# Row-wise stages of a decoder layer in 13 tiles of up to 126 rows instead of 16 tiles of 100

## The chip, the cores and the metric

The kernel runs on one core of one Trainium2 chip, as one program. The metric is device time in microseconds (us), lower is better. The engines are PE (TensorE, matrix products; PEld is its weight load), DVE (VectorE), ACT (ScalarE), POOL (GpSimd) and SP (SyncE, which here only issues DMAs). Each engine runs its own list of instructions in order and waits on semaphores.

## What is computed

One pre-norm decoder layer on 16 batches of 100 rows, width 512, in fp32:

```
x = x + self_attention(layernorm(x))        # 16 heads of 128, rotary, RMS-normed q and k, sink
x = x + cross_attention(layernorm(x), ctx)  # 16 heads of 32, keys and values from ctx
x = x + moe(layernorm(x))                   # RMS norm, router, 4 of 32 experts, plus a shared expert
```

The causal mask leaves only the first 100 of the 361 context rows in use. Attention works within a batch; layer norms, projections, the router and the shared expert work on each row by itself.

## The kernel before, in words

The program has four parts. **Joining**: two weight matrices of the output projection are multiplied into one per head (`join`), in 16 pieces. **Steps**: a software pipeline of 16 steps, one per batch (`step(b)` on every engine; steps 2 to 14 are a hardware loop in `pipeline`). **Behind the steps**: the leftovers of the pipeline, woven by hand into the shared expert. **Experts**: the 32 routed experts, two blocks of 128 gathered rows each, whose results are added into the output rows by indirect DMAs.

In step b the engines do the self-attention of batch b (stage A), the input norm, queries and keys of batch b+1 (stage Q), the cross attention of batch b-1 (stage X) and the norm, router and rank of batch b-2 (stage C). The order within a step is written out by hand for each engine. On PE it is: transposes of keys and queries (L532, L543), scores (L549, L552), `cross_queries` (transposed h2, context keys and values, the query product L453), `ln1_columns`, `cross_products`, `compress`, `queries` (L425, which waits until the cross scores have been copied out, `sx`), transposed probabilities and their product with the values (L584, L589), `normed_columns`, the output projection `project` (48 products of 512 columns, L382 to L384), with `router`, `cross_transposed` (L493, waits for `px_norm`), `cross_values` (L504) put between its last heads, `ranks`, and `cross_out` (L520), which waits for the copied columns `oxT`. Then the next step's first transpose waits for the scaled keys (`k_scaled`).

Most products with fp32 precision are made as three products of "high" and "low" halves (`split_product`). The high half is a copy by ACT, the low half a subtraction by DVE; both must be there before PE can start. Behind the steps the shared expert's weights ("sg", "su", "sd") and the normed rows in columns ("h0" to "h3", four groups of 400 rows) are split in this way (`split_high`, `split_low`); the first inner product of the shared expert waits for sg and h0, and its second half for su. Inner product n of 16 (`shared_inner`: PE makes gate and up products, ACT the SiLU, DVE the product, ACT the high and DVE the low half) feeds `shared_outer(g)`, 12 products of 512 columns for each tile of rows; DVE adds the kept base row (`shared_rows`) into one of two tiles `ytile`, and POOL stores it.

On DVE the parts that matter are the four scaled copies of the scores, max, shift, sum and norm of the softmax (L1272 to L1300), `cross_shifted` and `cross_normed` (L1189 to L1200), `rotate` (L1151 to L1158), `norms` (L1163, whose power of -0.5 POOL computes at L1483), `routed` (L1205 to L1229), the addition of the projected row (L1320) with its statistics, `scale_keys` (L1168) and `ranked` (L1234 to L1245). All 1600 rows stay in on-chip memory as `resid`, 16 tiles of 100 rows. POOL issues four indirect DMAs for each tile (`listed`), which write row numbers into the expert lists.

## Time and profile before

| what | value |
|---|---|
| median of 3 runs | 1219.54 us (1204.15, 1219.54, 1219.91) |
| the profiled execution | 1210.05 us |
| its span, first to last instruction | 1208.3 us |
| mean granted clock of PE | 0.983 of full speed |
| PE busy | 1146.3 us, 95% |
| DVE busy | 811.5 us, 67% |
| ACT busy | 595.0 us, 49% |
| first step starts, last step ends | 68.5 us, 726.2 us |
| first product of the first `shared_outer` | 783.1 us |

Times in the trace are us from the start of the span. A busy share is an average over parts with different limits. A row of the timeline merges neighbouring instructions of one kind; the bracket at its end says how long the engine was idle before it and what ended that.

### The profile page before, as it was taken

To read this page: it belongs to the slowest core of one execution; us is meant where nothing else is said; L and a number is where in the kernel's file an instruction comes from. 1 tells how busy PE (TensorE), PEld (TensorE's weight loads), DVE (VectorE), ACT (ScalarE), POOL (GpSimd) and SP (SyncE) were. 2 spreads that over 40 slices of the span, in tenths; PEclk is the share of its full clock that TensorE was granted. 3 is DMA by queue.
4 is the path that set the end of the run, shared out by engine and by line. 5 is a ranking of instruction groups with operands and counts; after the bars stand their busy time and mean duration, and the time that the engine had idled before them with its cause. 6 is when DMAs were issued, how large, how long until landed. Compare 5 with 4: busy or idle time off the path is not lost. (4 is left out here: it accounts for less than half of the span.)

```text
span 1208.3 us, 21017 instructions
## 1 busy us (share of the span) xinstructions
PE 1146.3 (95%) x7761; PEld 905.7 (75%) x7762; DVE 811.5 (67%) x1392; ACT 595.0 (49%) x1404; POOL 359.2 (30%) x279
## 2 busy tenths in 40 slices
PE   6989999999999999999999989899799999999993
PEld 3457677767776777777677758788699999898992
DVE  1355798789778978887898868532356666666660
ACT  1334564456446544654554435311156666666661
POOL 0011112211221122112122202222226676667653
PEclk9999999999999999999999988999989999999997
DMA  8450000000000000000000005122669999999964
GB/s 276 141 178 11 1 10 9 16 14 9 9 16 14 9 9 14 9 9 16 14 9 9 17 24 191 44 88 67 229 195 266 261 263 265 263 257 240 268 103 53
DMA packets 62598, 117.59 MB, mean 97 GB/s; under 512 B 10932, under 2 KB 14564, under 8 KB 62388
## 3 DMA queue, kind: packets, MB, share of 16 engines
q1 hardware_dynamic: 44820, 82.46, 20.2%
q0 software_dynamic: 17728, 34.44, 14.5%
q8 instruction: 33, 0.54, 0.2%
q14 instruction: 17, 0.14, 0.0%
HBM read 93.55 MB, written 28.13 MB: 101 GB/s over the span
## 5 line engine op out<-in xcount | busy, mean ns | idle before, releaser
L1483 POOL TENSOR_TENSOR rall<-qkv_var,phalf 100x17 f32<-100x17 f32 x16 | 49.1, 3071 | 404.1 <-DVE qkv_var L1163 404.1
L1561 POOL DMA_INDIRECT out_rows<-work,idx x64 | 119.6, 1868 | 110.0 <-issue 55.0
L382 PE MATMUL QS<-xh,wh 128*128 128x256 f32 x512 | 148.6, 290 | 0.0
L383 PE MATMUL QS<-xl,wh 128*128 128x256 f32 x512 | 146.0, 285 | 0.0
L384 PE MATMUL QS<-xh,wl 128*128 128x256 f32 x512 | 145.8, 285 | 0.0
L382 PE MATMUL W<-wch,oth 128*100 128x512 f32 x256 | 105.1, 410 | 0.0
L383 PE MATMUL W<-wcl,oth 128*100 128x512 f32 x256 | 100.6, 393 | 0.0
L384 PE MATMUL W<-wch,otl 128*100 128x512 f32 x256 | 100.4, 392 | 0.0
L382 PEld LDWEIGHTS QS<-xh,wh 128*128 128x128 f32 x512 | 99.4, 194 | 1.2
L383 PEld LDWEIGHTS QS<-xl,wh 128*128 128x128 f32 x512 | 99.4, 194 | 1.2
L384 PEld LDWEIGHTS QS<-xh,wl 128*128 128x128 f32 x512 | 99.2, 194 | 0.0
L1431 DVE TENSOR_TENSOR wl<-raw,wh 128x2048 fp32r<-128x2048 f32 (+1 forms) x48 | 84.5, 1761 | 12.1 <-ACT wh L799 10.9
L1483 POOL TENSOR_TENSOR rstd<-var,phalf 100x1 f32<-100x1 f32 (+1 forms) x48 | 30.2, 630 | 178.7 <-DVE var L1124 121.4
L1452 DVE TENSOR_TENSOR work<-work,QS 128x256 f32<-128x256 f32 x64 | 26.7, 417 | 72.5 <-ACT work L1063 54.5
L799 ACT ACTIVATE work<-W 128x400 f32<-128x400 f32 (+1 forms) x132 | 55.8, 508 | 31.8 <-PE W L584 31.7
L799 ACT ACTIVATE wh<-raw 128x2048 fp32r<-128x2048 f32 (+1 forms) x48 | 70.7, 1472 | 0.0
L453 PEld LDWEIGHTS W<-h2T,w_x 128*128 128x128 f32 x512 | 59.6, 192 | 8.1 <-ACT h2T L799 5.0
L1043 ACT ACTIVATE work<-W,wcol 128x512 f32<-128x512 f32 x64 | 40.5, 686 | 45.0 <-PE W L384 45.0
L1513 POOL DMA_INDIRECT expert_lists<-tok,slot x56 | 57.1, 1020 | 16.3 <-issue 16.3
L453 PE MATMUL W<-h2T,w_x 128*128 128x100 f32 x512 | 59.4, 274 | 0.0
L520 PE MATMUL W<-w_x,oxT 128*100 128x512 f32 x128 | 58.4, 599 | 0.0
L799 ACT ACTIVATE work<-QS 100x400 f32<-100x400 f32 (+1 forms) x76 | 41.7, 616 | 33.7 <-DVE work L1155 23.3
(223 smaller groups left out, 2880.9 us busy)
## 6 DMA issues: line engine op xcount, KB each, us to landing
raw<-in_w SPq DMA_DIRECT2D x24, 1024.0 KB
raw<-in_w SPq DMA_DIRECT2D x24, 512.0 KB
work<-in_w SPq DMA_DIRECT2D x8, 1024.0 KB
work<-in_w SPq DMA_DIRECT2D x8, 512.0 KB
hx_rows<-h3x SPq DMA_DIRECT2D x16, 212.5 KB
h_columns<-h3s SPq DMA_DIRECT2D x16, 200.0 KB, 1.9
h3T<-h_columns SPq DMA_DIRECT2D x4, 800.0 KB, 15.5
out_rows<-ytiles POOLq DMA_DIRECT2D x16, 200.0 KB, 2.5
```

Of the source, the lines that this page charges most:

```text
L382: mm(dst, ah, bh, start=start, stop=False)
L383: mm(dst, ah, bl, start=False, stop=False)
L384: return mm(dst, al, bh, start=False, stop=stop)
L453: last = mm(wb[1][:, T * i:T * (i + 1)], w_q[:, 512 * k + P * i:512 * k + P * (i + 1)], h2T[:, T * k:T * (k + 1)], start=k == 0, stop=k == ...
L520: last = mm(wb[3][0:T, :], oxT[:, T * k:T * (k + 1)], w_out[:, 512 * k:512 * (k + 1)], start=k == 0, stop=k == KC - 1)
L799: return fn(dst, src, ACT.Copy)
L1043: last = fn(Y[e % 2][:, 512 * j:512 * (j + 1)], wb[j][:, :], ACT.Copy, scale=wcol[e % RING][:, j:j + 1])
L1431: tt(wl[e % 2][:, c], slots_w[e % RING][:, c], wh[e % 2][:, c].bitcast(fp32), ALU.subtract).then_inc(m.wl, 1)
L1452: tt(ea[:, 256 * v:256 * (v + 1)], et[:, 256 * v:256 * (v + 1)], QS[:, 1280 + 512 * v:1536 + 512 * v], ALU.mult).then_inc(m.act, 1)
L1483: return nc.gpsimd.tensor_tensor(out=dst, in0=src, in1=phalf[:, 0:src.shape[1]], op=ALU.pow)
L1513: nc.gpsimd.indirect_dma_start(table, on_rows(slot[:, k:k + 1]), tok[:, :], None)\
L1561: nc.gpsimd.indirect_dma_start(out, on_rows(idx[:, NE * j + e:NE * j + e + 1]), Y[e % 2][:, 512 * j:512 * (j + 1)], None, compute_op=ALU.a ...
```

## The change

Everything that works on each row by itself behind the self-attention now takes tiles that cross the borders of batches. Five batches make four tiles of 124, 126, 126 and 124 rows; fifteen batches make 12 tiles, and the sixteenth is a tile of 100 rows, 13 in all (`pieces`). A tile can only be made once all its batches are there, so `tile_at(b)` gives the tile that is finished by batch b, and none for b = 0, 5 and 10. In step b now:

- self-attention of batch b, as before; its output columns go into a buffer of two batches (`oth3`, `otl3`), and `project` runs for `tile_at(b)`;
- norm 2 and the query product for `tile_at(b - 1)`, whose result ACT copies out in the pieces that belong to each batch;
- cross attention of batch b-2 (`context`, `cross_products` and so on), and `cross_out` for `tile_at(b - 2)`;
- norm 3, router and ranks for `tile_at(b - 3)`.

The hardware loop is gone, all steps are written out. Instead of `resid` there is a ring of four tiles; SP loads x twice (by batch for norm 1, by tile for the sum), stores each base tile to memory and loads the first nine back behind the steps. Constants for rows 100 to 125 are filled with 23 small DMAs (`spread`), behind the others, and POOL waits for all of them before its first step. POOL now issues the list DMAs of a tile ahead of the power for the next tile's norm 3. The shared expert's four groups have 3, 3, 3 and 4 tiles (376, 374, 374 and 476 rows). Its intermediate tile is one buffer (`joint`), so SiLU n waits for low half n-1. Behind the steps two cross attentions, two `cross_out` and three routers are left, instead of one, one and two.

```diff
+TT = 126
+NT = 13
+def tiles_of(b):
+    if b < 0:
+        return 0
+    return NT if b >= NB - 1 else 4 * (b // 5) + b % 5
+def tile_at(b):
+    return tiles_of(b) - 1 if 0 <= b < NB and tiles_of(b) > tiles_of(b - 1) else None
...
@@ tensor, step @@
+                c = b - 2
+                queried, listed, done = tile_at(b - 1), tile_at(b - 3), tile_at(b)
...
-                    project(b, range(0, 12))
+                if done is not None:
+                    project(done, b, range(0, 12))
...
+                if c >= 0:
+                    pe.wait_ge(s.px_norm, c + 1)
...
+                    cross_transposed(qb)
...
+                if tile_at(c) is not None:
+                    pe.wait_ge(s.oT, 4 * b + 4)
+                    cross_out(tile_at(c), c)
...
@@ gpsimd @@
-            pool.wait_ge(s.pad_st, 48)
-            pipeline(pool, step)
+            pool.wait_ge(s.pad_st, 48 + 16 * SPREAD)
+            for b in range(NB):
+                step(b)
...
@@ scalar, behind the steps @@
+            cross_exp(NB - 1)
+            shared_inner(2)
+            shared_inner(3)
+            columns_out(NT - 2)
...
@@ vector, behind the steps @@
-            normed(NB - 2, NB)
+            cross_shifted(NB - 2)
+            normed(NT - 3, NT)
             split_low("sg")
             split_low("h0")
-            cross_shifted(NB)
+            cross_normed(NB - 2)
+            routed(NT - 3)
             split_low("su")
```

**Place 1: DVE, just behind the steps.** `w_sgl`, `w_sul` are low halves of shared weights, `h3l` those of a group of rows; `mxx` belongs to `cross_shifted`, `denx` and `rx` to `cross_normed`, `lgs` starts `routed`. Before:

```order
L1181 SCALAR_TENSOR_TENSOR h3x<-work,rstd_90,normw 100x512
L1183 SCALAR_TENSOR_TENSOR resid<-work,rstd_90,resid 100x512
L1356 TENSOR_TENSOR w_sgl<-w_sh,w_sgh 128x2048
L1356 TENSOR_TENSOR h3l<-h3T,h3h 128x1600
L1189 TENSOR_REDUCE mxx<-work 100x16
L1191 TENSOR_TENSOR work<-work,mxx 100x1600
L1356 TENSOR_TENSOR w_sul<-w_sh,w_suh 128x2048
L1196 TENSOR_REDUCE denx<-work 100x16
```

After:

```order
L1384 TENSOR_REDUCE mxx<-work 100x16
L1386 TENSOR_TENSOR work<-work,mxx 100x1600
L1369 TENSOR_SCALAR work<-ring,mv_82 126x512
L1376 SCALAR_TENSOR_TENSOR h3x<-work,rstd_88,normw 126x512
L1378 SCALAR_TENSOR_TENSOR ring<-work,rstd_88,ring 126x512
L1567 TENSOR_TENSOR w_sgl<-w_sh,w_sgh 128x2048
L1567 TENSOR_TENSOR h3l<-h3T,h3h 128x1504
L1391 TENSOR_REDUCE denx<-work 100x16
L1393 RECIPROCAL rx<-denx 100x16
L1395 TENSOR_TENSOR work<-work,rx 100x1600
L1402 COPY lgs<-W 126x32
```

`cross_shifted` now stands ahead of norm 3 and of the first two splits, and `cross_normed` and the whole of `routed` (11 instructions from L1402 on) stand between the split of h0 and that of su.

**Place 2: DVE, around the first output rows of the shared expert.** `ytiles` are the finished rows, `rk` starts `ranked` of the last tile (and the counting at L1400 or L1623), `qpT` before and `h2T` now is the product of an inner product, `shl` its low half. Before:

```order
L1364 TENSOR_TENSOR qpT<-ckT,QS 128x400
L1370 TENSOR_TENSOR shl_161<-qpT,shh_155 128x400
L1234 TENSOR_TENSOR rk<-W,run 100x32
L1236 TENSOR_TENSOR run<-W,run 100x32
L1237 TENSOR_TENSOR pick<-oh,rk 100x128
L1243 TENSOR_REDUCE slot<-pick 100x4
L1245 COPY tok<-tokall 100x1
L1400 TENSOR_TENSOR rk<-run,runs 1x32
L1402 CAST cnt<-rk 1x32
L1404 TENSOR_REDUCE most<-rk 1x1
L1377 TENSOR_TENSOR ytiles<-resid,W 100x512 x4
L1364 TENSOR_TENSOR qpT<-ckT,QS 128x400
```

After:

```order
L1574 TENSOR_TENSOR h2T<-h2T,QS 128x374
L1578 TENSOR_TENSOR shl_159<-h2T,shh_155 128x374
L1588 TENSOR_TENSOR ytiles<-resid,W 124x512
L1588 TENSOR_TENSOR ytiles<-resid,W 126x512
L1436 TENSOR_TENSOR rk<-W,run 100x32
L1438 TENSOR_TENSOR run<-W,run 126x32
L1439 TENSOR_TENSOR pick<-oh,rk 100x128
L1446 TENSOR_REDUCE slot<-pick 100x4
L1448 COPY tok<-tokall 100x1
L1588 TENSOR_TENSOR ytiles<-resid,W 126x512
...
L1574 TENSOR_TENSOR h2T<-h2T,QS 128x374
L1578 TENSOR_TENSOR shl_160<-h2T,shh_156 128x374
```

`ranked` of the last tile stood ahead of all four rows of the first group, on PE too (`ranks` ahead of `shared_outer(0)`); now PE makes `ranks` behind `shared_outer(0)`, and on DVE `ranked` stands between the second row and the third. The third row, and inner product 7 behind it, come after. (The three instructions of the counting stand where the "..." is.)

**Place 3: PE, step 5, which finishes no tile.** `work,vS` is the product of probabilities and values of the self-attention, `W<-w_r` the router, `QS<-ident,work` the transposes of `cross_transposed`, `W<-work,cv` `cross_values`, `W<-w_x,oxT` `cross_out`, `kr` the keys of the next step.

Before (every step from 2 to 14; from the transposes of the cross attention on):

```order
L493 MATMUL QS<-ident,work 100x100 x16
L382 MATMUL W<-wch,oth 100x512
L383 MATMUL W<-wcl,oth 100x512
L384 MATMUL W<-wch,otl 100x512
L504 MATMUL W<-work,cv 32x100 x16
L382 MATMUL W<-wch,oth 100x512
L383 MATMUL W<-wcl,oth 100x512
L384 MATMUL W<-wch,otl 100x512
L513 MATMUL W<-chosen,tri 100x32
L514 MATMUL W<-chosen,ones 100x32
L520 MATMUL W<-w_x,oxT 100x512 x4
```

After, in step 5 (with the semaphores that each waits for):

```order
L702 MATMUL W<-work,vS 128x400 [waits pT] x3
L494 MATMUL W<-ident,h3x 128x126 [waits ln3_h,rank_used,oT]
L494 MATMUL W<-ident,h3x 128x126 x3
L587 MATMUL W<-w_r,h3s 126x32 [waits h3s,oT]
L587 MATMUL W<-w_r,h3s 126x32 x3
L596 MATMUL QS<-ident,work 100x100 [waits q_out,q_ssq,px_norm]
L596 MATMUL QS<-ident,work 100x100 x15
L607 MATMUL W<-work,cv 32x100 [waits cv,pxT,oT,h3s]
L607 MATMUL W<-work,cv 32x100 x15
L619 MATMUL W<-chosen,tri 126x32 [waits h3s,chosen,oxT]
L627 MATMUL W<-w_x,oxT 126x512 [waits oxT,oT]
L640 MATMUL QS<-ident,kr 128x100 [waits pxT,q_rot,k_scaled]
```

The 48 products of `project` that stood between and around these (42 ahead of the first row of before) are gone in steps 0, 5 and 10; the waits are the same.

## Rows read from the trace of the kernel before

**Rows 1.** Windows: stretch, us, busy of PE, PEld, DVE, ACT, POOL, clock, DMA share, GB/s

```profile
68.48:105.85 37.37, 33.88 (x169) 22.55 (x169) 20.48 (x34) 15.65 (x56) 3.89 (x3) 1.00 0.23 62
105.85:145.94 40.09, 39.88 (x291) 29.27 (x292) 28.50 (x42) 21.35 (x65) 4.59 (x4) 1.00 0.01 3
352.90:394.30 41.40, 41.26 (x307) 30.34 (x306) 34.75 (x68) 22.04 (x68) 8.95 (x8) 1.00 0.04 12
...
726.20:783.10 56.90, 50.48 (x334) 45.56 (x334) 39.65 (x71) 28.66 (x39) 12.48 (x10) 0.94 0.28 101
```

**Rows 2.** Timeline of PE in the step from 352.90: start, us, instructions

```profile
354.71 0.87 PE L552 MATMUL QS<-kT,work 128*100 128x100 f32 x8
...
358.40 1.06 PE L442 MATMUL W<-ctxT,w_x 128*128 128x100 f32 x8
...
360.15 3.71 PE L453 MATMUL W<-h2T,w_x 128*128 128x100 f32 x32
363.70 0.51 PE L402 MATMUL W<-ident,work 100*128 100x100 f32 x4
364.05 0.84 PE L464 MATMUL QS<-mask,identb 100*100 100x400 bf16 x4
...
365.71 1.14 PE L414 MATMUL W<-h1T,w_comp 128*128 128x100 f32 x8
...
371.84 1.54 PE L584 MATMUL W<-ident,work 100*100 100x100 f32 x16
...
376.30 0.46 PE L382 MATMUL W<-wch,oth 128*100 128x512 f32 x1
...
384.65 0.81 PE L484 MATMUL W<-w_r,h3s 128*100 128x32 f32 x8
...
390.80 3.66 PE L520 MATMUL W<-w_x,oxT 128*100 128x512 f32 x8
```

**Rows 3.** Timeline of DVE and POOL in the same step

```profile
382.88 1.83 DVE L1200 TENSOR_TENSOR work<-work,rx 100x1600 f32<-100x1600 f32 x1
...
393.01 0.35 DVE L1168 SCALAR_TENSOR_TENSOR kr<-kr,rall,wqk 100x128 f32<-100x128 f32 x1
...
384.96 3.07 POOL L1483 TENSOR_TENSOR rall<-qkv_var,phalf 100x17 f32<-100x17 f32 x1 [22.84 <-DVE qkv_var L1163]
```

**Rows 4.** PE restarting in step 15 and behind the steps, and a window there

```profile
701.27 2.90 PE L584 MATMUL W<-ident,work 100*100 100x100 f32 x16 [4.66 <-DVE work L1300]
...
736.49 1.54 PE L484 MATMUL W<-w_r,h3s 128*100 128x32 f32 x8 [2.33 <-ACT h3s L799]
...
736.00:738.00 2.00, 1.51 (x9) 1.51 (x10) 1.97 (x3) 2.00 (x3) 0.00 (x0) 0.56 1.06 406
```

**Rows 5.** Timeline of DVE in step 0

```profile
76.24 0.54 DVE L1129 TENSOR_SCALAR work<-resid,mv,rstd 100x512 f32<-100x512 f32 x1
...
100.41 0.18 DVE L1163 TENSOR_SCALAR qkv_var<-ssq 100x17 f32<-100x17 f32 x1 [3.34 <-ACT QS L847]
```

**Rows 6.** Timeline of SP: first and last of 14 constants, and the last zero fill

```profile
2.35 0.41 SPq L283 DMA_DIRECT2D ident<-in_c_ident  x1
...
9.81 0.34 SPq L283 DMA_DIRECT2D normw<-in_normw  x1
...
62.79 0.59 SPq L298 DMA_DIRECT2D out_rows<-in_c_zero  x1
```

**Rows 7.** Timeline of DVE just behind the steps

```profile
734.42 1.81 DVE L1356 TENSOR_TENSOR h3l<-h3T,h3h 128x1600 fp32r<-128x1600 f32 x1
...
739.74 2.28 DVE L1356 TENSOR_TENSOR w_sul<-w_sh,w_suh 128x2048 fp32r<-128x2048 f32 x1
...
748.42 0.39 DVE L1229 TENSOR_REDUCE h3x<-ohw 100x32 f32<-100x128 f32 x1
```

**Rows 8.** Timeline of DVE: last of the ranks, and third row of the first group

```profile
783.32 0.14 DVE L1245 COPY tok<-tokall 100x1 int32<-100x1 int32 x1
...
795.02 0.69 DVE L1377 TENSOR_TENSOR ytiles<-resid,W 100x512 f32<-100x512 f32 x1 [5.39 <-DMA out_rows<-ytiles]
```

More of the change, by code:

```diff
@@ new lines, in step @@
+                pe.wait_ge(s.v, b + 1)
+                for i in range(4):
+                    pe.wait_ge(s.pT, 4 * b + i + 1)
+                    mm(wb[i][:, 0:QW], vS[:, :], T16[0:T, QW * i:QW * (i + 1)], start=True, stop=True)\
+                        .then_inc(s.o_ps, 1)
+                if listed is not None:
+                    pe.wait_ge(s.oT, 4 * b + 2)
+                    normed_columns(listed)
+                if done is not None:
+                    project(done, b, range(0, 12))
@@ L605, in step @@
+                if listed is not None:
+                    pe.wait_ge(s.oT, 4 * b + 3)
+                    router(listed)
+                if done is not None:
+                    project(done, b, range(12, 14))
+                if c >= 0:
+                    pe.wait_ge(s.px_norm, c + 1)
+                    if more:
                         pe.wait_ge(s.q_ssq, 2 * (b + 2))
@@ L636, in _ @@
             pe.wait_ge(s.ld_wx, 64)
-            pipeline(pe, step)
+            for b in range(NB):
+                step(b)
             def shared_inner(g, f):
@@ new lines, in _ @@
+            pe.wait_ge(s.sx, NB - 1)
+            shared_inner(0, 0)
+            pe.wait_ge(s.px_norm, NB - 1)
+            pe.wait_ge(s.lg, NT - 2)
+            pe.wait_ge(s.cv, NB - 1)
+            cross_transposed(wb)
+            shared_inner(0, 1)
+            cross_values(NB - 2)
+            pe.wait_ge(s.oxT, NB - 1)
+            ranks(NT - 3)
+            cross_out(NT - 2, NB - 2)
+            context(NB - 1, wb[0])
+            pe.wait_ge(s.sh_act, 2)
+            cross_products(NB - 1)
@@ L1231, in ranked @@
[L1231 to L1241 removed]
+                dve.wait_ge(s.top_exp, i + 1)
@@ L1334, in step @@
-                if do.X:
-                    cross_added(b - 1)
+                if listed is not None:
+                    routed(listed)
+                if done is not None:
+                    projected(done)
+                if more:
+                    scale_keys(b + 1)
+                if listed is not None:
+                    ranked(listed)
+                if done is not None:
+                    ln2_apply(done, tiles_of(b - 3))
+                if tile_at(c) is not None:
+                    cross_added(tile_at(c))
@@ L1348, in _ @@
             joined(range(13, 14))
-            pipeline(dve, step)
+            for b in range(NB):
+                step(b)
             def split_low(n):
@@ L1381, in _ @@
+            cross_shifted(NB - 2)
+            normed(NT - 3, NT)
             split_low("sg")
             split_low("h0")
-            cross_shifted(NB)
+            cross_normed(NB - 2)
+            routed(NT - 3)
             split_low("su")
-            cross_normed(NB)
-            routed(NB - 2)
+            shared_inner(0)
+            shared_inner(1)
+            ranked(NT - 3)
+            cross_added(NT - 2)
+            cross_shifted(NB - 1)
+            normed(NT - 2, NT)
             split_low("h1")
-            for n in range(3):
-                shared_inner(n)
```

1206 lines of the change are left out of this document (662 added, 544 removed).

## The prediction

> **What bounds the kernel now.** I read the windows by stage first, then the timeline of PE in one step, then those of DVE, POOL and SP, and last the part behind the steps. In the windows [rows 1] a step of the hardware loop lasts 41.40 us and PE is busy for 41.26 of it, while DVE has 34.75: the steps are PE's, with 6.65 us of DVE to spare. Steps 0 and 1 are shorter (37.37 and 40.09) as they lack work of other batches. Behind the steps it is different: of 56.90 us PE works 50.48, at a mean clock of 0.94, so it waits 6.4. So the change is worth its PE work in the steps only as far as nothing else ends a step, and behind the steps the order on DVE and ACT counts.
>
> The timeline of PE [rows 2] gives the price of each part by the start of one row and of the next: the query product 360.15 to 363.70 = 3.55; context 358.40 to 360.15 = 1.75; cross products 364.05 to 365.71 = 1.66; `project` has 36 products between 376.30 and 384.65, 0.23 each, so 48 are 11.0; the router 0.65; `cross_out` 12 products, 3.5 (its last row 3.66 with its tail). `shared_outer` has 12 products of the same 512 columns, 2.8 a tile.
>
> **Part 1: fewer row tiles.** Three tiles fewer save PE 3 × (11.0 + 3.55 + 3.5 + 2.8) = 62.6 us. Are the wider tiles dearer? In `project`, `cross_out` and `shared_outer` the rows are the stationary side and 512 columns move, so they are not. In the query product the rows move: 126 instead of 100 columns. The 32 products of L453 (100 columns, 128 stationary) take 3.55, 111 ns each; the 8 of L552 (same 100 moving, 100 stationary) read 0.87, less the same 0.16 of overlap 0.71, 89 ns each [rows 2]. The pace goes with the stationary width and so with the load, which hides 26 more columns: I take 0; the other bound is 26% of 3.55, 0.9 a tile, 12 in all.
> The Trainium skill ("TensorE: Matmul & The Clock Gate", section "Back-to-back issue gap") prices an isolated product by its columns alone, N/2.4 plus some 2.5 ns; by that rule 26 columns would add 11 ns to each, 0.35 a tile and 4.5 in 13 tiles, to the sum below. The two rows above speak against it here.
>
> The router (L484) moves 32 columns with the rows stationary; I take 0.2 more a tile, 0.65 to 0.84. DVE's and ACT's operations handle rows in parallel and stay. Naively 60 us go. Now each step.
>
> **Step 0** (no `project`, -11.0). The keys for step 1 don't come earlier by that: L1163 at 100.41 waited 3.34 for ACT's squares, then POOL's power takes 3.07 [rows 3], then scaling 0.35: 104.1 against the step's end 105.85, -1.7 at best. Against that stand 23 small DMAs at the end of SP's list. The 14 constants took 2.35 to 9.81, 0.53 each [rows 6], so 23 take about 12.5; behind the zero fill at 62.79 + 0.59 [rows 6] the last is issued at 76 and lands near 78. POOL waits for all; DVE's first norm instruction in step 0 was at 76.24 [rows 5], so about +2. I take +0.2, bounds -1.7 and +6 (POOL's 3.07 once for the start and once more in front of the keys).
>
> **Steps 1 to 3.** Step 1 has no cross attention: 40.1 falls to 36.8 (-3.3). Step 2 has cross attention but no `cross_out`: -3.5, yet keys come 2.4 behind the end of `project` (L1320's sum and statistics before L1168 at 393.01 [rows 3], while PE's step ended at 394.30, with `cross_out` from 390.80 as cover): 39.5, -1.9. Step 3 has no router: -1.1.
>
> **Steps 5 and 10** (no `project`, -11.0). Here the cover goes. `cross_normed` L1200 is on DVE from 382.88 to 384.71, so done 31.8 us into the step [rows 3], behind L1300, rotation and the norms in DVE's list, whose order stays. PE without `project` is at the transposes about 26 us into the step, waits 5.7, then transposes 1.3 (as L584 [rows 2]), copy 0.5, values 0.8, copy 0.5, `cross_out` 3.5: 38.9. And after such a wait the clock is low: in step 15 PE waited 4.66 for DVE and the same L584 then took 2.90 [rows 4] against 1.54 [rows 2]; behind the stop of 2.33 at 736.49 the eight L484 took 1.54 against 0.81 [rows 2], in a window at 0.56 [rows 4]: near the 1.2 GHz level. Price of a restart: from 1.4 (that row alone) to 3.4 (56.90 × 0.06 = 3.4, the whole loss behind the steps [rows 1]); 2.8 taken, 0 as lower bound. So 41.5: of 11 us nothing is left.
>
> **The steps after.** 6 and 11 have no query product, -3.55, but ACT's copies of `sx` and the norm rows for the next queries come when they came: 2.2 of wait, -1.3. 7 and 12 have no `cross_out`, and the keys end 2.4 behind `project`: -0.6. 8 and 13 without a router: -1.1. 4, 9, 14 have all of it, with wider routers and ranks: +0.3. Step 15 stays. Loop: 0.2 - 3.3 - 1.9 - 1.1 + 0.3 + 2 × (0.1 - 1.3 - 0.6 - 1.1 + 0.3) = -5.8 - 5.2 = -11.0. Bounds: -20 (no clock loss and no late start) and 0 (+6 in step 0, +2 in each of 5 and 10).
>
> **Part 2: behind the steps, up to the first outer product** (56.9 before).
> PE's work: a second cross attention and a router move behind the steps: context 1.75, products 1.66, transposes 1.3, values 0.8, `cross_out` 3.5, a router 0.84 and its transposes 0.35: 10.2; seven inner products of 24 products with some 25 columns less (an estimate from 0.23 for 512 columns: 0.011 each): -1.7. Sum +8.5.
> Waits: this is where DVE's order bites.
> - The first cross attention's products, h2 in columns, the query product and a router follow each other with copies between and nothing to fill them: 3.7 (some 7 hops of 0.5).
> - h0's low half is L1356 at 734.42 + 1.8 [rows 7]. Now `cross_shifted` (two operations of 1.8) and norm 3 of the last tiles stand ahead of it in DVE's list, and 10 us more of PE beside it: +2.2.
> - su's low half (739.74, 2.28 long [rows 7]) stood ahead of `cross_normed` and `routed`; now it stands behind them. `cross_normed` is 3.9, `routed` 2.9 (up to L1229 at 748.42 [rows 7]). PE has 4.2 us of sg products meanwhile: it waits 5.3. Queued behind su's split on DVE are the next h and shared products, which PE doesn't yet need.
> - The copy of `oxT` 0.9; `sx` of batch 15 1.6; the transposed norm rows of tile 11, which ACT copies only behind `shared_inner(3)`, which waits for DVE, in `cross_normed` of batch 15: 5.6; `oxT` again 0.9; 0.2.
> Together 20.4 of waits, and three of them are long enough for cold restarts: 1.7, 2.5 and 2.6 by what PE has behind each until the clock is back, 6.8. Off go the 6.4 of idle and the 3.4 of clock that were there. 20.4 + 6.8 - 9.8 = +17.4, and with the work +25.9: the first outer product comes 82.8 behind the steps. Bounds: +8.5 (waits as before) and +32 (each restart 3.4, and one more).
>
> **Part 3: the shared expert's rest** (87.6 before). Three tiles of outer products less: -8.3. Four inner products of 476 columns instead of 400, 0.8 more each, and five of 374, 0.24 less each: +2.0. New: rows 1 and 2 of the first group go out, the third needs the store of row 0, which POOL issues. POOL's list runs through `listed`, which waits for `ranked`; before, the last `tok` was at 783.32 and the third row came at 795.02, 11.7 later, after 5.39 of waiting for the DMA [rows 8]. Then this lay beside four outer tiles. Now `ranks` are behind them on PE: with T the start of `shared_outer(0)`, 3 tiles end at T + 8.4, `ranked` at T + 12.1, the third row at T + 24, product 7 on DVE at T + 25.3; PE has inner products up to T + 16.8: waits 8.5, and a restart 2.7. Sum -8.3 + 2.0 + 8.5 + 2.7 = +4.9. Bounds: -6 (the store is issued first) and +8. The experts' part has the same work: 0.
>
> **The sum.** -11.0 + 25.9 + 4.9 = +19.8 on the span of 1208.3: 1228.1, with 1.75 around the span 1229.9, so 1230. Against its own 1210.05 that is +1.6%. The median before is 1219.54; the profiled execution is 9.5 lower and one of the three runs 6 lower still. I add nothing for that. A measurement of this kernel can tell about 2% from no change.
>
> **Rivals.**
> *The clock falls at the short waits too* (slower). Place: the waits of 1.5 to 2.3 us in steps 6 and 11 and behind the steps; price 3.4 each; from the second on the result is past 1234 (+2% of 1210.05). For it: the 0.56 behind a stop of only 2.33 us [rows 4]. Against it: the mean of 0.94 behind the steps with several short stops [rows 1]. Four of them: 1230 + 14 = 1244. Chance 0.36.
> The Trainium skill ("TensorE: Matmul & The Clock Gate", section "HAM oscillation — how this bites in real kernels") says that a kernel which alternates work and waits can be put back to the low clock over and over, which would be this rival. The window at 0.56 agrees, the 0.94 only in part.
> *The waits behind the steps stay as they were* (ACT and DVE have slack, and PE's extra 10 us cover the splits): -11.0 + 8.5, and -6.3 in the third part without its stop: -8.8, 1201. For it: DVE has 39.65 of 56.90 [rows 1], a third free. Against it: su's split is plainly behind 6.8 us of DVE. Chance 0.12, of it 0.04 beyond 2%.
> *PE bounds all* and the order hides everything: the naive 60 go, 1150. For it: PE has 41.26 of 41.40. Against it: L1200, done at 31.8, can't move up by PE's finishing sooner, as what feeds it starts with the step. Chance 0.09.
>
> **How the numbers follow.** Forecast 1230, its own range 1212 to 1234, 0.43. Faster by over 2%: 0.09 + 0.04 = 0.13; slower by over 2%: 0.36; within 2%: 0.43 + 0.08 = 0.51. Loop bounds (-20 to 0), the tail (+8.5 to +32) and the rest (-6 to +8) at their joint ends give 1192 to 1250; the range is 1190 to 1250, with the rival at 1244 inside and the naive one outside.
>
> **What would show it.** In the profile after: steps 5 and 10 as long as their neighbours, with PE idle near 26 us into them for L1395 and a clock under 0.9; steps 4, 9, 14 near 41.7; a PE stop of 5 for `w_sul`; one of some 8 us before inner product 8 for a DVE row that waits for a DMA of `out_rows`; the query product (L554) at 3.6 a tile. Wrong if steps 5 and 10 last under 36, if the 126-column query product takes over 4.2, or if the first `shared_outer` begins less than 70 us behind the steps.

## The result

The changed kernel is slower: its median is 1253.86 us in 4 runs (1250.63 to 1259.86), that of the kernel before 1219.53 us in 4 runs (1204.15 to 1219.91), ratio 1.032, 95% interval 1.023 to 1.041. The profiled execution took 1250.83 us with a span of 1249.0, 40.7 more than the span before. The forecast was 1230, the range ended at 1250.

| stage, us | before | forecast | after |
|---|---|---|---|
| up to step 0 | 68.5 | same | 69.6 |
| steps 0 to 15 | 657.7 | -11.0 | -0.7 |
| behind the steps, up to the first outer product | 56.9 | +25.9 | +35.1 |
| up to the first product of the experts | 94.4 | +4.9 | +7.9 |
| experts | 330.8 | 0 | -2.7 |
| span | 1208.3 | +19.8 | +40.7 |

The page of the changed kernel, first the head, then the granted clock in 40 slices:

```profile
span 1249.0 us, 19308 instructions
...
PE 1117.2 (89%) x7407; PEld 902.0 (72%) x7408; DVE 783.2 (63%) x1299; ACT 603.3 (48%) x1405; POOL 348.4 (28%) x270
...
PEclk9996899997999999799999888888989999999997
```

PE is busy for 29 us less than before (1146.3), and yet the end comes 41 us later. The clock is now low in many slices, in the steps too; its mean is 0.941 against 0.983. A busy PE at the low clock also counts as busy, so the saved work is more than 29 us. If each busy us at a granted clock of 0.50 is counted as a half (an estimate from the instructions and the clock of both traces), PE's work is 1134.7 us before and 1071.7 after: 63 less, so the work that the forecast took off is really gone.

The windows of the changed kernel, in the columns of [rows 1]: steps 1 to 5, 7 and 8, then the part behind the steps and the shared expert's rest.

```profile
105.37:143.49 38.12, 32.08 (x153) 24.28 (x153) 20.16 (x35) 14.90 (x54) 3.88 (x3) 0.86 0.01 3
143.49:185.83 42.34, 39.90 (x283) 32.02 (x284) 27.98 (x41) 22.05 (x66) 4.25 (x4) 0.92 0.05 13
185.83:226.10 40.27, 40.09 (x291) 30.56 (x292) 28.52 (x42) 21.69 (x66) 4.58 (x4) 1.00 0.07 19
226.10:267.80 41.70, 41.51 (x306) 31.76 (x305) 34.61 (x67) 22.46 (x69) 4.92 (x4) 1.00 0.11 30
267.80:311.53 43.73, 36.16 (x258) 26.76 (x257) 33.00 (x62) 22.75 (x69) 12.77 (x10) 0.80 0.12 31
...
351.53:392.35 40.82, 38.44 (x298) 30.27 (x297) 33.65 (x62) 22.21 (x69) 8.57 (x8) 1.00 0.11 30
392.35:434.28 41.93, 41.75 (x292) 32.18 (x292) 29.21 (x47) 21.96 (x66) 9.91 (x8) 0.96 0.08 19
...
726.61:818.64 92.03, 69.88 (x450) 60.79 (x448) 50.93 (x87) 38.65 (x51) 16.29 (x15) 0.81 0.29 93
818.64:913.56 94.92, 82.17 (x377) 70.38 (x377) 25.15 (x54) 16.60 (x26) 24.84 (x36) 0.93 0.34 118
```

Steps 3, 4 and 7 came as forecast (40.3, 41.7, 40.8), and so did step 6 (40.0). Step 5, which makes no `project`, takes 43.7, more than a step of before that makes one, at a clock of 0.80. Step 2 was to take 39.5 and took 42.3, step 8 41.9 instead of 40.3, with PE busy nearly throughout (41.75 of 41.93) at a clock of 0.96: there the loss is no wait but slow work. Behind the steps the clock is 0.81, where it was 0.94.

PE's timeline in step 5, in the columns of [rows 2]:

```profile
293.48 1.88 PE L587 MATMUL W<-w_r,h3s 128*126 128x32 f32 x8 [2.08 <-ACT h3s L941]
...
299.56 2.90 PE L596 MATMUL QS<-ident,work 100*100 100x100 f32 x16 [4.19 <-DVE work L1395]
...
303.14 1.56 PE L607 MATMUL W<-work,cv 100*32 100x100 f32 x32 [0.69 <-ACT work L941]
...
305.32 0.28 PE L619 MATMUL W<-chosen,tri 126*126 126x32 bf16 x1 [0.62 <-ACT oxT L941]
...
305.55 6.14 PE L627 MATMUL W<-w_x,oxT 128*126 128x512 f32 x8
311.53 0.25 PE L640 MATMUL QS<-ident,kr 100*128 100x100 f32 x1
```

L596 starts 31.8 us into the step, as L1200 bound it in [rows 3]. But the low clock begins before it, behind the first stop: from 293.5 to 310.5 the granted clock is 0.50, and the router's eight products take 1.88 after a wait of only 2.08 (0.81 in [rows 2]). What follows runs at half pace too: the 16 transposes take 2.90 (1.54 for 16 transposes in [rows 2]), the values 1.56, and `cross_out`, from 305.55 to the end of the step, 6.0 instead of 3.5.

The stops of PE behind the steps, one row each:

```profile
734.70 6.62 PE L554 MATMUL W<-h2T,w_x 128*128 128x100 f32 x32 [3.98 <-ACT h2T L941]
...
754.12 0.68 PE L474 MATMUL QS<-h3h,w_suh 128*128 128x376 f32 x1 [4.79 <-DVE w_sul L1567]
...
774.82 0.68 PE L474 MATMUL QS<-h3h,w_sgh 128*128 128x376 f32 x1 [2.32 <-ACT work L1032]
...
788.98 1.86 PE L587 MATMUL W<-w_r,h3s 128*124 128x32 f32 x8 [3.69 <-ACT h3s L941]
...
811.95 0.60 PE L494 MATMUL W<-ident,h3x 100*128 100x100 f32 x4 [3.63 <-DVE h3x L1376]
...
845.47 0.68 PE L474 MATMUL QS<-h3h,w_sgh 128*128 128x374 f32 x1 [9.90 <-DVE h2T L1574]
```

The 32 products of L554 take 6.62 here against 3.71 for the same shape in [rows 2]; the single L474 of 376 columns takes 0.68, which in the shared expert at full clock is 0.33.

DVE shows where two of these come from: the low half of su stands right behind `routed`, and the third row of the first group waits 13.41 us for a DMA.

```profile
751.50 0.37 DVE L1427 TENSOR_REDUCE h3x<-ohw 126x32 f32<-126x128 f32 x1
751.79 2.28 DVE L1567 TENSOR_TENSOR w_sul<-w_sh,w_suh 128x2048 fp32r<-128x2048 f32 x1
...
821.69 0.55 DVE L1574 TENSOR_TENSOR h2T<-h2T,QS 128x374 f32<-128x374 f32 x1
827.84 0.55 DVE L1578 TENSOR_TENSOR shl<-h2T,shh 128x374 fp32r<-128x374 f32 x1 [5.61 <-ACT shh L941]
...
830.35 0.14 DVE L1448 COPY tok<-tokall 100x1 int32<-100x1 int32 x1
843.90 0.69 DVE L1588 TENSOR_TENSOR ytiles<-resid,W 126x512 f32<-126x512 f32 x1 [13.41 <-DMA out_rows<-ytiles]
```

The last `tok` comes 11.7 us behind the first outer product (818.64); before, it came 0.2 behind it [rows 8]. And it isn't only the place of the ranks: product 6 (L1574, L1578) stands ahead of them. Its low half L1578 waits for the high half, which ACT makes only at 827.29, when PE is through with the first outer group at 827.03, 8.4 us behind its start.

POOL shows what I had not counted: norm 3's power for tile 12 stands behind four list DMAs, and L494 at 811.95 waited for it.

```profile
802.71 1.35 POOL L1720 DMA_INDIRECT expert_lists<-tok,slot  x1 [29.60 <-DVE tok L1448]
...
807.58 2.15 POOL L1720 DMA_INDIRECT expert_lists<-tok,slot  x1 [0.30 <-issue]
809.75 0.74 POOL L1701 TENSOR_TENSOR rstd<-var,phalf 100x2 f32<-100x2 f32 x1
```

The variance was ready at 806.1. Where later runs put the power ahead of the lists (e4_tail, e8_tail2), a stop of 2.27 stays there, so the lists account for some 1.4 of the 3.63.

### The profile page after: what moved, and what is told of

Same layout as the page of the kernel before. It is cut to its first block and busy times, and to the rows that moved or that the text cites. A ratio compares the mean times of both kernels' runs of the same rounds, so it can differ in the third digit from the quotient of the medians.

```text
span 1249.0 us, 19308 instructions
## 1 busy us (share of the span) xinstructions
PE 1117.2 (89%) x7407; PEld 902.0 (72%) x7408; DVE 783.2 (63%) x1299; ACT 603.3 (48%) x1405; POOL 348.4 (28%) x270
## 5 line engine op out<-in xcount | busy, mean ns | idle before, releaser
L474 PE MATMUL QS<-xh,wh 128*128 128x256 f32 x512 | 147.7, 289 | 0.0
L1782 POOL DMA_INDIRECT out_rows<-work,idx x64 | 115.0, 1797 | 112.1 <-issue 57.4
L474 PEld LDWEIGHTS QS<-xh,wh 128*128 128x128 f32 x512 | 98.5, 192 | 1.2
L1720 POOL DMA_INDIRECT expert_lists<-tok,slot x52 | 60.5, 1164 | 120.8 <-DVE tok L1448 105.2
L1649 DVE TENSOR_TENSOR wl<-raw,wh 128x2048 fp32r<-128x2048 f32 (+1 forms) x48 | 84.5, 1760 | 12.7 <-ACT wh L941 12.5
L474 PE MATMUL W<-wch,oth 128*124 128x512 f32 (+2 forms) x208 | 86.9, 418 | 0.0
L475 PE MATMUL W<-wcl,oth 128*124 128x512 f32 (+2 forms) x208 | 82.0, 394 | 0.0
L476 PE MATMUL W<-wch,otl 128*124 128x512 f32 (+2 forms) x208 | 81.9, 394 | 0.0
L941 ACT ACTIVATE work<-W 100x400 f32<-100x400 f32 (+1 forms) x136 | 59.4, 506 | 35.3 <-PE W L697 31.6
L1670 DVE TENSOR_TENSOR work<-work,QS 128x256 f32<-128x256 f32 x64 | 26.8, 418 | 68.0 <-ACT work L1251 38.7
L1701 POOL TENSOR_TENSOR rstd<-var,phalf 100x1 f32<-100x1 f32 (+5 forms) x42 | 26.2, 627 | 132.5 <-DVE var L1311 108.3
L941 ACT ACTIVATE work<-QS 100x400 f32<-100x400 f32 (+1 forms) x72 | 40.7, 622 | 41.8 <-DVE work L1346 25.5
L1231 ACT ACTIVATE work<-W,wcol 128x512 f32<-128x512 f32 x64 | 40.6, 685 | 40.4 <-PE W L476 40.4
L554 PEld LDWEIGHTS W<-h2T,w_x 128*128 128x128 f32 x416 | 51.0, 201 | 10.8 <-ACT h2T L941 5.8
L662 PEld LDWEIGHTS QS<-kT,work 128*100 128x100 f32 x512 | 58.0, 175 | 0.5
L517 PE MATMUL QS<-w_up,hqT 128*100 128x512 f32 x128 | 58.1, 596 | 0.2
```

Of the source, the lines that this page charges most:

```text
L474: mm(dst, ah, bh, start=start, stop=False)
L475: mm(dst, ah, bl, start=False, stop=False)
L476: return mm(dst, al, bh, start=False, stop=stop)
L517: mm(qb[i][0:T, :], hqT[:, :], w_up[:, 512 * i:512 * (i + 1)], start=True, stop=True).then_inc(s.q_ps, 1)
L554: last = mm(wb[1][:, n * m4:n * (m4 + 1)], w_q[:, 512 * k + P * m4:512 * k + P * (m4 + 1)], h2T[:, n * k:n * (k + 1)], start=k == 0, stop= ...
L662: last = mm(qb[i][0:T, T * j:T * (j + 1)], T16[:, T * h:T * (h + 1)], kT[:, :], start=False, stop=j == QH - 1)
```

## The experiments

Two theories stood against each other. **Order**: the time is lost in stops behind the steps that the new order on DVE, ACT and POOL makes. **Clock**: the low clock behind each stop, the short ones in the steps too, eats what the fewer tiles save. The measure of most runs is the length of a stage in their own trace, since the time of a single run depends on the chip: in these sessions the median of the kernel before was between 1202.7 and 1213.7 us. The stages by run (from the first transpose of step 0 to that of step 15; from there to the first outer product; from there to the last outer product):

| kernel | steps 0 to 14 | step 15 and behind | outer products |
|---|---|---|---|
| before | 615.6 | 99.1 | 87.3 |
| changed | 614.4 | 134.6 | 94.7 |
| e1_su | 615.1 | 127.7 | 94.9 |
| e2_inner7 | 614.8 | 131.0 | 91.1 |
| e3_fill | 603.6 | 131.8 | 95.0 |
| e4_tail | 621.0 | 120.5 | 94.2 |
| e6_fill2 | 600.6 | 135.6 | 94.8 |
| e7_idx | 614.8 | 134.7 | 84.6 |
| e9_ranks | 614.8 | 136.8 | 91.5 |
| e12_ranks_rows | 615.3 | 136.8 | 88.8 |
| e8_tail2 | 601.7 | 123.3 | 81.9 |
| e11_order | 616.3 | 120.7 | 84.6 |
| e10_tail3 | 597.9 | 111.3 | 83.9 |
| e13_best | 599.8 | 117.3 | 83.4 |

**e1_su.** The low half of su ahead of `cross_normed` and `routed`:

```diff
             split_low("h0")
+            split_low("su")
             cross_normed(NB - 2)
             routed(NT - 3)
-            split_low("su")
```

> Edit: behind the steps, DVE makes the low half of su right behind that of h0, ahead of the cross softmax's norm and the router of the same place. Theory (DVE's order is what PE waits for): the stop of 4.79 us for w_sul at 754.12 in the changed kernel goes, the first outer product comes 4 to 5 us earlier relative to the end of the steps, and some 1 to 2 us of low clock with it. Rival (other copies and norms are late anyway): the cross softmax of batch 14 comes 2.3 later, PE waits there instead, the first outer product moves by less than 1.5 us.

The stop for `w_sul` fell to 0.64, and one of 1.68 for the cross softmax (L1395) came in its place. The second stage was 127.7 against 134.6. But ACT's copy L1032 there waited 3.46 us in the changed kernel and 1.00 in this run. It waited as short in e2 and e3, whose edits don't touch this stage and whose stage is 131.0 and 131.8: like with like the edit gave 3.3 to 4.1 us. That is more than the rival's 1.5 and less than the 4 to 5 and some low clock that the theory gave: the order costs time here, but less than expected.

**e2_inner7.** Product 7 ahead of the third row:

```diff
                     ranked(NT - 1)
+                    shared_inner(7)
                     shared_rows(GROUPS[0][2:])
...
-                    shared_inner(7)
```

> Edit: behind the steps, DVE makes shared product 7 ahead of the third output row instead of behind it. Theory (product 7 is late only because it is queued behind a row that waits for a store behind the list DMAs): PE's stop of 9.90 us at 845.47 goes, the shared expert's rest falls from 95.0 to about 84 us. Rival (the third row's buffer holds PE back as well, through the sums that wait to be taken): a stop of 5 us or more appears at the outer products of the second group, and less than 4 us are gained.

Only 3.6 us were gained. The stop split in two, which the rival's "less than 4" had, though the new stops are in other places: PE now waited for product 9 and then for the transposed lists.

```profile
848.71 0.37 PE L843 MATMUL QS<-ident,ixf 64*128 64x64 f32 x1 [3.38 <-DVE h2T L1574]
854.98 0.68 PE L474 MATMUL QS<-h3h,w_sgh 128*128 128x374 f32 x1 [5.90 <-DVE idx L1636]
```

**e3_fill.** Products without use where PE waits:

```diff
+            def fill(bank, n):
+                for _ in range(n):
+                    mm(bank, wch[:, 0:128], wch[:, 512:1024], start=True, stop=True)
...
+                    fill(wb[0], {5: (7, 16), 10: (7, 16)}.get(b, (0, 0))[0])
                     router(listed)
...
+                    fill(wb[0], {5: (7, 16), 10: (7, 16)}.get(b, (0, 0))[1])
                     pe.wait_ge(s.px_norm, c + 1)
...
+                    if b == 1:
+                        fill(wb[3], 12)
                     ln1_columns(b + 1, wb[0])
...
+                if b in {0: 44, 1: 8, 2: 8, 7: 8, 12: 8}:
+                    pe.wait_ge(s.oT, 4 * b + 4)
+                    fill(wb[3], {0: 44, 1: 8, 2: 8, 7: 8, 12: 8}[b])
```

> Adds PE products without use (each 512 columns, about 0.23 us, result never read) where PE waits in the loop: 44 at the end of step 0, 8 at the ends of steps 1, 2, 7 and 12, 12 in step 1 ahead of the norm columns, 7 and 16 in steps 5 and 10 ahead of router and cross transposes. They lie inside the waits. Theory (the low clock behind a stop is what eats the gain): step 5 falls from 43.7 to 39 to 40 us, step 8 from 41.9 to 40.3, step 1 from 38.1 to 34 to 36, step 2 from 42.3 to 40; the loop as a whole gets 12 to 18 us shorter. Rival (the stops themselves are the cost, or the clock is a matter of total load): each step stays within 0.5 us of what it was, or grows by the products that don't fit.

Step 1 fell to 33.6, step 2 to 39.2, step 8 to 40.4. More work for PE made the loop 10.8 us shorter, and what changed in the trace is the clock (step 8: 1.00 instead of 0.96). Step 2 by itself proves little: in e1 and e2, which have no such products, it is 39.2 too, and step 3 is 41.9 in its place. But the two together take 79.4 here, 81.1 there and 82.6 in the changed kernel. The loop gained less than the 12 to 18 expected: step 0 was 38.7 here against 35.8 in the changed kernel's trace, and step 5 stayed at 42.55. Its windows of 2 us and PE's rows say why:

```profile
296.00:298.00 2.00, 0.91 (x17) 0.99 0.00 0
298.00:300.00 2.00, 1.40 (x33) 0.50 0.36 80
300.00:302.00 2.00, 2.00 (x5) 0.50 0.62 190
```

```profile
297.83 1.48 PE L607 MATMUL W<-work,cv 100*32 100x100 f32 x32 [1.09 <-ACT work L952]
299.91 0.29 PE L619 MATMUL W<-chosen,tri 126*126 126x32 bf16 x1 [0.60 <-ACT oxT L952]
...
300.14 5.99 PE L627 MATMUL W<-w_x,oxT 128*126 128x512 f32 x8
```

The stops for `px_norm` (1.35), for `pxT` (1.09) and for `oxT` (0.60) follow each other. From 298.0 on, behind the first two, the clock is at its lower level, 1.2 GHz, and `cross_out` takes 5.99 again.

**e6_fill2** fills those too (the edit against e3_fill).

```diff
-                    fill(wb[0], {5: (7, 16), 10: (7, 16)}.get(b, (0, 0))[1])
+                    fill(wb[0], {5: (7, 20), 10: (7, 20)}.get(b, (0, 0))[1])
                     pe.wait_ge(s.px_norm, c + 1)
...
+                    fill(wb[0], 4 if b in (5, 10) else 0)
                     cross_values(c)
...
+                    fill(wb[0], 2 if b in (5, 10) else 0)
                     pe.wait_ge(s.oxT, c + 1)
```

> As e3_fill, and in steps 5 and 10 more products without use: 20 instead of 16 ahead of the cross transposes, 4 ahead of cross_values, 2 ahead of the ranks. In e3_fill step 5 fell only to 42.55 us, with the clock at 0.50 from 298 to 304 us while cross_out ran (5.99 us instead of 3.7). Theory (each stop in the step puts the clock down anew, so the price of the clock in a step without project is up to 4 us, not 2.8): step 5 falls to 39.5 to 40 us with a clock of 1.00. Rival (something other than PE ends step 5, keys or lists): it stays over 41.5.

```profile
262.89:302.48 39.59, 38.90 (x291) 28.94 (x290) 33.00 (x62) 22.32 (x69) 10.87 (x9) 1.00 0.13 32
383.90:424.34 40.44, 40.27 (x292) 30.58 (x293) 29.29 (x47) 21.72 (x66) 9.90 (x8) 1.00 0.08 20
```

Step 5 takes 39.59 at full clock, step 8 40.44. So the low clock cost 4.1 in step 5, 1.5 in step 8 and on balance 13.9 in the loop (614.4 to 600.6). That balance has 3.0 against it from step 0, and 2.3 from steps 6 and 11, which took 40.7 and 41.6: their stop ahead of L494 grew from 1.44 to 2.1, and in step 11 the clock fell behind it (mean 0.96).

**e4_tail.** The edits of e1 and e2, and:

```diff
@@ tensor and scalar, behind the steps @@
+            norm2_columns(NT - 1)
             context(NB - 2, wb[3])
...
             shared_inner(2)
+            columns_out(NT - 2)
             shared_inner(3)
@@ gpsimd, in the steps and behind them @@
+                    ln3(tile_at(b - 2))
                     listed(tile_at(b - 3))
```

> Both edits before, and behind the steps also: norm 2's columns of the last tile first on PE and ACT; ACT copies the norm-3 columns of tile 11 ahead of SiLU 3; POOL computes a tile's norm-3 power ahead of the list DMAs, in the steps as well. Theory (order behind the steps costs 35 of the 45 us lost): time falls by 18 to 28 us, to 1222 to 1235; PE stops of 3.98, 4.79, 3.69, 3.63 and 9.90 us go or fall under 1.5. Rival (PE's added work there and the low clock in the loop are what costs): less than 10 us are gained, 1240 or more.

It measured 1247.30 us (1245.81 to 1254.53), ratio to before 1.029 (1.021 to 1.037): the gain was missed, and the number is in the rival's range, 1240 or more. The traces split it up: 14.1 us came off behind the steps, so the order there did cost time. But steps 6 and 11 went from 40.0 to 43.4 and 43.5, and the stop for the lists stayed. In step 6 of this kernel POOL's power for norm 1 stands behind lists that now wait for the other power (the rows are POOL's and PE's):

```profile
317.95 0.98 POOL L1720 DMA_INDIRECT expert_lists<-tok,slot  x1 [0.30 <-issue]
318.95 0.59 POOL L1701 TENSOR_TENSOR rstd<-var,phalf 100x1 f32<-100x1 f32 x1
...
320.18 0.93 PE L494 MATMUL W<-ident,work 100*128 100x100 f32 x4 [2.43 <-DVE work L1320]
```

The stop is 2.43, 1.0 more than in the changed kernel, and from 319.9 on the granted clock is 0.50 for 6.8 us, where it stayed at full there: the rest of the 3.4 is the clock's. So the changed kernel's order on POOL, lists ahead of the power, is right in the steps and costs only behind them.

**e7_idx.** As e2_inner7, with the lists transposed behind inner product 11, and DVE's copy of them between products 10 and 11:

```diff
-                if g == 1:
-                    pe.wait_ge(s.sh_act, 10)
+                if g == 2:
+                    pe.wait_ge(s.sh_act, 11)
                     pe.wait_ge(s.idx, 1)
                     tr(qb[0][:, 0:2 * NE], ixf, ident[0:2 * NE, 0:2 * NE]).then_inc(s.ix_T, 1)
```

> As e2_inner7, and the transposition of the expert lists is made behind inner product 11 instead of behind the second group of outer products. In e2_inner7 the stop of 9.90 us had become two, 3.38 for product 9 and 5.90 for the lists' index. Theory (both the third row and the index wait for the lists of the last tile, which are written late since its ranks are late): with both moved behind other work the shared expert's rest falls from 94.8 to 84 to 87 us. Rival (PE is short of work there whatever the order): over 90 us.

84.6 instead of 94.7, with 1.01 and 0.99 left of the two stops: both were there because the third row and the lists' index came late, and other work could stand ahead of them.

**e9_ranks** put the ranks back ahead of the first outer product on PE and `ranked` ahead of the first row on DVE.

```diff
-                shared_outer(g)
                 if g == 0:
                     ranks(NT - 1)
+                shared_outer(g)
...
                     shared_inner(6)
-                    shared_rows(GROUPS[0][0:2])
                     ranked(NT - 1)
-                    shared_rows(GROUPS[0][2:])
+                    shared_rows(GROUPS[0])
```

> Undoes one part of the change: ranks of the last tile ahead of the first outer product on PE, and its list positions ahead of the first output row on DVE, as in the kernel before. Theory (the new place of the ranks makes the stop): the last tok comes some 8 us earlier relative to the first outer product, the stop of 9.90 us falls to 0 to 3, against a new wait of 1 to 3 us for the router's result ahead of the first outer product; net 4 to 8 us gained from the end of the loop to the last outer product. Rival (the first group's three tiles instead of four are too short a cover wherever the ranks stand): the stop stays over 6.

Missed: the stop was 8.84, as the rival said (over 6), and `tok` came at 831.80, 10.5 us behind the first outer product, though PE had made the ranks at 821.16. My reading in the forecast, that the place of the ranks is what makes the lists late, does not hold by itself. Between them stood product 6, whose low half (L1578) came at 830.48 after a wait of 7.77.

**e12_ranks_rows** therefore puts product 6 behind the rows as well, the order of before in full (the edit against e9_ranks):

```diff
                 if g == 0:
-                    shared_inner(6)
                     ranked(NT - 1)
                     shared_rows(GROUPS[0])
...
+                    shared_inner(6)
                     shared_inner(7)
```

> e9_ranks gained nothing: its last tok still came at 831.80, 10.5 us behind the ranks on PE, since product 6 stood ahead of it on DVE, and the halves of product 6 wait for the end of the first outer group. Here the whole order of the kernel before is put back: on PE ranks of the last tile ahead of the first outer product, on DVE its list positions, then the three rows, then products 6 and 7. Theory (product 6 ahead of the ranks holds DVE until the first group is done, and with it lists, stores and the third row): tok comes within 1 us of the first outer product, the stop of 9.90 us falls under 3, and the rest takes 84 to 88 us instead of 94.7, with up to 2 us more ahead of it. Rival (three tiles of cover are too few whatever the order): a stop of 6 us or more.

DVE's rows and PE's:

```profile
823.83 0.14 DVE L1448 COPY tok<-tokall 100x1 int32<-100x1 int32 x1
...
839.25 0.69 DVE L1588 TENSOR_TENSOR ytiles<-resid,W 126x512 f32<-126x512 f32 x1 [10.56 <-DMA out_rows<-ytiles]
...
840.92 0.65 PE L474 MATMUL QS<-h3h,w_sgh 128*128 128x374 f32 x1 [6.07 <-DVE h2T L1574]
```

Half right. `tok` now comes 1.7 behind the first outer product and the stage is 88.8, 5.9 shorter than in the changed kernel. But a stop of 6.07 stays, which meets the rival's "6 us or more": from `tok` to the third row the lists and stores take 15.4 us (11.7 in [rows 8]), and the first group has three tiles to cover it, one less, or 2.8 us. Of the 3.7 us more, 3.5 are one pause of POOL between two list DMAs, 3.77 instead of 0.30, which nothing in the trace explains. So this run shows no more than that the order alone does not remove the stop; this order without that pause was not measured.

**e8_tail2 and e11_order.** e8 joins e1, e6, e7 and of e4 what lies behind the steps; e11 is e8 without the products without use.

> e1_su, e6_fill2 and e7_idx together, and of e4_tail what lies behind the steps (norm 2's columns first, the norm columns of tile 11 ahead of SiLU 3, power ahead of the lists behind the steps), not its order of POOL in the steps, which made steps 6 and 11 3.4 us longer. Theory (the parts add up: 16 in the loop, 10 behind it, 8 in the rest): 1249 - 34 = 1215, 1208 to 1222, no longer distinguishable from the kernel before. Rival (what is gained in one place is lost at the next wait): 1228 or more.

> e8_tail2 without the products without use: only the order behind the steps and of the index. Theory (order and clock add up, the clock in the loop is worth 14 to 15 us): 1225 to 1232, steps 5 and 10 at 43.8 and 8 and 13 at 41.9 again. Rival (the products without use do more than keep the clock, or the stops behind the steps grow with them): under 1220 or over 1237.

e8 measured 1215.31 us (1208.88 to 1217.97), ratio to before 1.011 (1.004 to 1.018); e11 1228.81 us (1220.92 to 1231.91), ratio 1.018 (1.010 to 1.025). Both medians lie where the theory put them, though e8 is still distinguishable from the kernel before, and its parts were not those expected: 12.7 in the loop, 11.3 behind it and 12.8 in the rest, instead of 16, 10 and 8. That the sum came out is in part luck. In the loop the difference of the two runs is 14.5 us and the clock's on balance; in e11 steps 5 and 8 take 43.8 and 41.9 again.

**e10_tail3 and e13_best.** The order behind the steps written out once more. The main edits of e10:

```diff
@@ vector, behind the steps @@
+            normed(NT - 3, NT)
             cross_shifted(NB - 2)
-            normed(NT - 3, NT)
...
+            cross_shifted(NB - 1)
             cross_added(NT - 2)
-            cross_shifted(NB - 1)
@@ tensor, behind the steps @@
             cross_products(NB - 1)
+            cross_out(NT - 2, NB - 2)
...
             router(NT - 2)
+            shared_inner(1, 0)
             pe.wait_ge(s.px_norm, NB)
```

> e8_tail2 with the order behind the steps written out once more: norm 3 of tile 10 ahead of the cross softmax of batch 14 (and its power ahead of the lists in the last step), the products of batch 15 ahead of cross_out, one inner product more between the router of tile 11 and the cross transposes of batch 15, inner product 6 ahead of norm 3's columns of tile 12; and 8 products without use in steps 6 and 11 ahead of the norm columns. Theory (what is left behind the steps are stops of 4.76, 3.88, 1.37 and 2.27 us and the low clock behind them): from the start of step 15 to the first outer product 123.3 falls to 110 to 115, the time to 1200 to 1208, within 1% of the kernel before on the same chip. Rival (the chain from the cross scores through softmax to the norm is too long for the PE work there is): 120 or more, the time as e8_tail2.

> e10_tail3 with the order of e12 for ranks, rows and products 6 and 7. Theory: in e10 the rest takes 83.9 us, of which 2 to 3 are stops of this kind; the wait for the router's result ahead of the first outer product costs about as much: within 2 us of e10_tail3, 1198 to 1203. Rival (the lists being early lets the gathers and the experts start sooner): 1196 or less.

e10 measured 1200.82 us in 12 runs (1198.37 to 1203.68) against 1208.64 for the kernel before on the same chip, ratio 0.996 (0.993 to 0.998). e13, which adds the order of e12, measured 1205.31 us in 12 runs (1199.03 to 1212.40) against 1207.57, ratio 0.996 (0.992 to 0.999). Both lie 0.4% under the kernel before, clear of no change by their intervals and far inside 2%. e10's trace is 52 us shorter than the changed kernel's, and 50.6 of them lie in the three stages of the table. The windows of e10: step 6, then the two parts behind the steps.

```profile
302.76:342.76 40.00, 39.67 (x278) 29.16 (x277) 34.29 (x66) 21.42 (x66) 7.84 (x7) 1.00 0.11 29
710.20:778.88 68.68, 59.65 (x449) 50.55 (x449) 49.26 (x86) 36.48 (x50) 17.18 (x13) 0.95 0.37 122
778.88:863.10 84.22, 80.36 (x379) 68.54 (x379) 26.63 (x55) 18.43 (x28) 27.64 (x39) 0.98 0.40 128
```

The part behind the steps is 68.7 us with PE busy for 59.7 of it, against 92.0 and 69.9 in the changed kernel. The early lists of e13 didn't pay: PE waited 3.69 for `chosen` ahead of the first outer product, and behind the steps it took 6 us more than e10. Neither the 1198 to 1203 expected for e13 nor the rival's 1196 came; but its ratio to the kernel before is the same as e10's, so the two are not told apart.

## Why the prediction was wrong

The likeliest case was 1230, within 2% of before; measured is 3.2% more. Most waits were foreseen in their places; the size of one cost, the low clock behind them, wasn't. It is the rival that I gave 0.36 which happened: the clock falls at the short stops too. It had 1244 as its time, and even that was short.

*Naive saving and width: right.* The query product with 126 columns takes what it took with 100. PE's groups, of the changed kernel in step 4 (the columns: busy us, mean ns of one, idle us before):

```profile
L554 PE MATMUL W<-h2T,w_x 128*128 128x126 f32 x32 | 3.7, 275 | 0.0
```

and of the kernel before in the step of [rows 2]:

```profile
L453 PE MATMUL W<-h2T,w_x 128*128 128x100 f32 x32 | 3.7, 274 | 0.0
```

By the starts of the rows the changed kernel takes 3.57 us for the 32 (233.24 to 236.81), 112 ns each, as the forecast had 3.55 and 111. The 63 us of work that went, by the estimate above, are near the 62.6 of the sum.

*Steps.* The step that failed is "And after such a wait the clock is low ... 2.8 taken". In the loop it was charged once in steps 5 and 10 and nowhere else. Measured against e6 it is 4.1 in step 5, as the clock falls already behind the stop of 2.08 ahead of the router, which the forecast didn't have as a stop, and the transposes, the values and nearly all of `cross_out` come before it is back; and the keys that are 2.2 us late, which I had as a wait at the end of steps 2, 7 and 12 and not of step 1, put the clock down at the start of steps 2, 8 and 13. The terms: step 1 +1.3 over the forecast, step 2 +2.8, steps 5 and 10 +2.2 and +2.3, steps 8 and 13 +1.6 each, step 0 -1.8, together 10.0 of the 10.3 missed. With the stops filled the loop is 15.0 shorter than before in e6 (615.6 to 600.6) and 17.7 in e10, and my sum without its price for the clock was about -17. What I said of the waits holds: `px_norm` at 31.8, the keys 2.2 to 2.3 late, steps 3, 4, 6, 7 and 9 within 0.2. Step 1 doesn't bear the sum out: at full clock it takes 33.6 (e3, e6), 3.2 less than the 36.8 forecast, so the low clock cost more there than the 1.3 by which the time was missed.

The Trainium skill ("TensorE: Matmul & The Clock Gate", section "HAM oscillation — how this bites in real kernels") describes a kernel in which every round of work begins at the low clock because a wait came before it. The trace agrees with it in steps 5 and 10 and behind the steps, where the mean clock is 0.80 and 0.81; but behind the stop of 2.27 at 185.83 the clock stayed at full.

*Behind the steps.* +35.1 instead of +25.9. The work is as counted. The stops add up to 22.2 us (20.4 forecast): w_sul 4.79 against 5.3, `oxT` 0.83 and 0.82 against 0.9 twice, `sx` 2.32 against 1.6, the router of tile 11 3.69 against 5.6; not foreseen was the 3.63 for norm 3 of tile 12, behind POOL's lists. The failing term is again the clock: of 69.88 us that PE is busy, 50.5 - 3.4 + 8.5 = 55.6 is its work at full pace, so 14.3 went to the low clock, where I had 6.8. I had put it behind three stops; the granted clock was 0.50 in five stretches there, 34 us in all.

*The shared expert's rest.* +7.4 up to the last outer product instead of +4.9, from the stop of 9.90 (8.5 forecast), the clock behind it, and a second fall of the clock at 901.0, at a stop of 2.13. Its place was right, its cause only in part: I put the late lists down to the place of the ranks, but e9 and e12 show product 6 to hold DVE ahead of them. Even with both put back a stop of 6.07 stayed, which the missing tile and POOL's pause between two list DMAs account for together.

*Step 0.* +2 for the 23 small DMAs was wrong. POOL went on at 77.17, when the last had landed (78 in the forecast), but that power was not what the step waited for: the keys came 11.9 us behind PE's last product, and the step took 35.8: the -1.7 that the forecast had as "at best" is nearly what came. In the other runs it took 37.4 to 39.0, where its first products were at a clock of 0.50; so part of the 1.8 is luck of this trace.

## What to carry to other kernels

Work taken off a busy engine is worth nothing where it was the cover of a chain on other engines: the time stays, the engine now stops, and on TensorE each stop can be paid a second time in the clock. Here that was 14 us in the loop and as many behind it, against 63 us of work removed. Count that price for short stops too, and when a change leaves short stops in a loop, try products without use in them: it is a quick measurement of the clock's share, and here it was also a gain. And when a pipeline is made deeper, its drain must be ordered anew on all engines: 23 us lay there, more than everything that the fewer tiles gave in the loop.

## What the runs showed of the hardware that I had not expected

- Stops of 2.1 to 2.3 us lower the clock in some places and not in others. In the changed kernel the stop of 2.26 at 143.49 was followed by 6.6 us at 0.50, and step 2 took 42.3; in e1_su the same stop of 2.26 cost nothing there (step 2 39.2), but the one after it did (step 3 41.9 instead of 40.3). The two steps together differ by 1.5. Stops of 1.44 ahead of L494 in steps 6 and 11 were not followed by slow work in any run (0.56 for the 4 transposes).
- Two stops of 1.35 and 1.09 us with little work between them lowered it as well (e3_fill, clock 0.50 from 298.0 us on). The third, of 0.60, came when it was already low, so whether it had to be filled too is not shown.
- ACT's copy L1032 behind the steps started 1.00 us after its idle time began in some runs and 3.46 in others, with "remote" as what released it in the changed kernel. The DMAs moved 389 GB/s there and 381 in e1_su, where it was 1.00, so their traffic alone does not tell the two apart. What it waits for stays open. So does the 3.77 us that POOL stood between two list DMAs in e12.
- The experts' part, which no edit touched, took between 322 and 334 us in the traces. Differences of a few us in the whole time are therefore read from stages, not from single runs.
